# Row maxima turned by VectorE in 32x32 blocks, a later first block for them, another order of the split products, and VectorE's low parts one slot later

## The reference, cut to what matters

```python
x  = L0_attn_z                                  # (4, 1024, 128)
xn = layernorm(x)
# attention over xn: second layernorm with weights, 16 heads of width 8
qkv    = (zn @ W_qkv + b_qkv)
scores = einsum('bhqd,bhkd->bhqk', q, k) * 8 ** -0.5
s      = xn + softmax(scores) @ v ... @ W_proj + b_proj
# experts over xn: 8 experts of hidden size 512, the two best of 8 weighted
h   = gelu(einsum('td,edh->eth', xn, W1) + b1)
ffn = einsum('etd,te->td', einsum('eth,ehd->etd', h, W2) + b2, weights)
out = x + s * silu(ffn)
```

## Time and profile before

| | |
|---|---|
| median of 3 runs | 1103.75 us (1102.54 to 1105.91) |
| profiled execution | 1103.0 us |
| its span, first to last instruction | 1101.2 us |
| mean granted TensorE clock | 0.988 |
| TensorE busy | 1029.3 us, 93% |
| VectorE busy | 883.7 us, 80% |
| ScalarE busy | 866.9 us, 79% |
| GpSimd busy | 368.0 us, 33% |

### The profile page before, as it was taken

The page is one execution under the profiler, slowest core; times in us unless marked ns, Lnnn a source line. Parts: engine busy times, 40 slices in busy tenths (PEclk is TensorE's granted clock), DMA queues, the critical chain, the costliest instruction groups (busy, mean ns, idle before and its releaser), DMA issues.

```text
span 1101.2 us, 17451 instructions
## 1 busy us (share of the span) xinstructions
PE 1029.3 (93%) x5865; PEld 444.1 (40%) x5897; DVE 883.7 (80%) x1589; ACT 866.9 (79%) x1190; POOL 368.0 (33%) x555
## 2 busy tenths in 40 slices
PE   4998999999999999999999999999999999999997
PEld 3675666666666666664222222122222121122222
DVE  5647877787878787765999899989998998899943
ACT  6876667676767677666898998989898989798985
POOL 4786656657666667554001000001000001000010
PEclk9999999999999999999999999999999999999998
DMA  6432221414142232324212221212112221122102
GB/s 183 123 99 68 66 83 31 120 30 121 31 107 50 64 80 51 97 51 120 51 44 53 55 53 39 68 40 54 42 52 51 56 53 42 51 53 54 25 24 82
DMA packets 99410, 72.02 MB, mean 65 GB/s; under 512 B 21693, under 2 KB 83834, under 8 KB 99322
## 3 DMA queue, kind: packets, MB, share of 16 engines
q1 hardware_dynamic: 99322, 70.92, 24.5%
HBM read 53.12 MB, written 15.46 MB: 62 GB/s over the span
## 4 chain that ended last, share of the span: by engine, by line
PE 34%; ACT 8%; DVE 7%; issue 2%; SPq 1%; DMA 0%; POOL 0%; ACTq 0%; DVEq 0%; POOLq 0%
PE psum L1055 17%; PE psum L1034 8%; ACT p_ring L869 8%; PE psum L999 7%; DVE neg_max_half L1318 7%; PE psum L1084 1%; ACT o_sb L860 1%; DMA den<-o_sb 0%; SPq L469 0%; PE psum L1098 0%; PE psum L1010 0%; SPq L473 0%; DVE neg_max_rest L1327 0%; DVE y L1379 0%; POOL h_lo L685 0%
## 5 line engine op out<-in xcount | busy, mean ns | idle before, releaser
L869 ACT ACTIVATE p_ring<-psum 128x1024 f32<-128x1024 f32 x512 | 494.8, 1026 | 59.7 <-PE psum L1034 54.3
L1318 DVE TENSOR_REDUCE neg_max_half<-psum 128x1 f32<-128x512 f32 x768 | 481.6, 681 | 44.5 <-PE psum L999 36.7
L1055 PE MATMUL psum<-p_ring,v_sb 128*9 128x512 f32 x2048 | 269.2, 598 | 0.4 <-ACT o_sb L860 0.3
L823 ACT ACTIVATE h_hi<-psum,cols 128x512 fp32r<-128x512 f32 x192 | 132.4, 690 | 132.2 <-PE psum L949 131.2
L999 PE MATMUL psum<-k_max_stack,q_max_stack 48*128 48x512 bf16 x768 | 202.2, 380 | 16.6 <-DVE neg_max_half L1318 16.3
L1336 DVE TENSOR_REDUCE neg_max_half<-psum 128x1 f32<-128x512 f32 x256 | 169.3, 683 | 51.7 <-PE psum L985 45.0
L685 POOL TENSOR_TENSOR h_lo<-h_split,h_hi 128x512 fp32r<-128x512 f32 x128 | 165.1, 1294 | 135.4 <-ACT h_split L826 135.2
L1034 PE MATMUL psum<-q_stack,k_stack 51*128 51x512 bf16 x1024 | 200.0, 386 | 3.4 <-ACT p_ring L869 2.2
L635 POOL CAST neg_max_parts<-neg_max_rest 128x16 bf16<-128x16 f32 x32 | 6.3, 197 | 493.6 <-DVE neg_max_rest L1327 493.5
L1034 PEld LDWEIGHTS psum<-q_stack,k_stack 51*128 51x128 bf16 x1024 | 49.5, 93 | 299.2 <-ACT p_ring L869 276.2
L947 PE MATMUL psum<-xn_t_hi,w_hi 128*128 128x512 f32 x256 | 144.8, 566 | 0.7 <-DVE neg_max_half L1336 0.5
(11 more groups left out here) (129 smaller groups left out, 957.5 us busy)
## 6 DMA issues: line engine op xcount, KB each, us to landing
expert_w_bc<-expert_w_dram SPq DMA_DIRECT2D x64, 256.0 KB, 5.1
k_rows_dram<-qk_parts SPq DMA_DIRECT2D x24, 256.0 KB, 3.1
q_max_stack<-q_rows_dram SPq DMA_DIRECT2D x64, 96.0 KB, 2.5
k_max_stack<-k_rows_dram SPq DMA_DIRECT2D x64, 96.0 KB, 2.5
q_stack<-q_rows_dram SPq DMA_DIRECT2D x64, 96.0 KB, 2.4
k_stack<-k_rows_dram SPq DMA_DIRECT2D x64, 96.0 KB, 2.5
q_rows_dram<-qk_parts SPq DMA_DIRECT2D x8, 384.0 KB, 2.6
xz<-in_L_attn_z_dram SPq DMA_DIRECT2D x8, 256.0 KB, 3.2
```

Source lines behind the costliest of these rows:

```text
L823: act.activation(hh[:, (g * HS + j) % HR, :], up, ACT.Gelu, bias=col(C_B1 + i))\
L869: act.activation(p_sb[:, n % PR, a, :, :].rearrange("p h t -> p (h t)"), scores_bank[s % 2], ACT.Exp, scale=SCALE).then_inc(S("P"), 1)
L1055: i = pe.matmul(o_bank[at:at + VR, :], v_sb[:, b * KT + kt, 2 * (p % PB) + hh, :], p_sb[:, n % PR, a, hh, :], start=(kt == 0), stop=(kt == ...
L1318: dve.tensor_reduce(mx[:, p % MXR, c, hh * NT + t:hh * NT + t + 1], ring_bank(("max", u)), AX.X, ALU.max, negate=True).then_inc(S("R"), 1)
```

## The change

1. TensorE's turn of the maxima and ScalarE's copy go. VectorE turns the parts in 32x32 blocks from SBUF to SBUF (`max_turn`): the parts' tile is padded to four parts, 64 columns, so each partition block of 32 holds the transpose of its own tokens. The store writes 128 rows of 128 bytes. The load puts the pieces in order: six DMAs per pair, each of 32 pieces of 64 bytes, instead of two. The turns take no bank of the ring any more, and stand three blocks, or seven slots, after the pair's last reduction.
2. The 768 maxima products of the attention stage are spread over blocks 2 to 239 instead of 0 to 239. The zeroing of the O bank moves into the last group of the expert stage.
3. Of the three split products, low weights by high data comes first, so that the two products of the same high weights follow one another.
4. VectorE's low parts of h stand one slot later in its plan.

The second identity (`ident_b`) and its waits go as well. The diff, cut to its core:

```diff
-    NM = 2 * PARTS * NT
...
-    m_dram = nc.dram_tensor("neg_max_dram", (PAIRS, NM, P), BF16, kind="Internal").ap()
+    m_dram = nc.dram_tensor("neg_max_dram", (PAIRS, P, 2 * VC), BF16, kind="Internal").ap()
...
-        nmp = sb("neg_max_parts", [P, 2, 2, PARTS, NT], BF16)
-        nmT = sb("neg_max_t", [NM, 2, P], BF16)
+        nmp = sb("neg_max_parts", [P, 2, 2, VC // NT, NT], BF16)
+        nmT = sb("neg_max_t", [P, 2, 2 * VC], BF16)
...
+        MAX_FROM = 2
...
-            upto = [min(len(SINGLES), -(-((n + a) * len(SINGLES)) // MAX_BLOCKS)) for a in range(2)]
+            upto = [min(len(SINGLES), -(-max(0, n + a - MAX_FROM) * len(SINGLES) // (MAX_BLOCKS - MAX_FROM)))
+                    for a in range(2)]
...
-        turn_at = {done_block(p) + 2: p for p in range(EARLY_PAIRS, PAIRS)}
+        turn_at = {done_block(p) + 3: p for p in range(EARLY_PAIRS, PAIRS)}
...
-            turns = []
-            if n in turn_at:
-                turns.append(("mT", turn_at[n]))
-            return halves, turns
+            return halves
...
-        EARLY_TURN = [2 * HT + 2, 2 * HT + 28, 3 * HT + 26, 4 * HT + 26, 5 * HT + 26, 6 * HT + 26, 7 * HT + 5, 8 * HT + 1]
         EARLY_MIN = [d + 2 for d in EARLY_DONE]
+        EARLY_TURN = [d + 7 for d in EARLY_DONE]
...
-            kind, k = RING[at][:2]
-            if kind == "max":
-                eng.wait_ge(S("R"), EARLY + k + 1)
-            else:
-                eng.wait_ge(S("mTc"), k + 1)
+            eng.wait_ge(S("R"), EARLY + RING[at][1] + 1)
...
-            sp.wait_ge(S("mTc"), p + 1)
+            sp.wait_ge(S("mT"), p + 1)
...
-                sp.dma_start(q_s[HALF * hh + QROWS:HALF * hh + SROWS, slot, :],
-                             m_dram[p].rearrange("(h i t) c -> h i (t c)", h=2, i=PARTS)[hh])\
-                    .then_inc(S(f"m_ld{slot}"), 16)
+                src = m_dram[p, :, VC * hh:VC * (hh + 1)].rearrange("(b i t) c -> i t b c", b=P // VC, t=NT)
+                for i in range(PARTS):
+                    row = HALF * hh + QROWS + i
+                    sp.dma_start(q_s[row:row + 1, slot, :].rearrange("a (t b c) -> a t b c", t=NT, c=VC), src[i:i + 1])\
+                        .then_inc(S(f"m_ld{slot}"), 16)
...
+            pool.memset(nmp[:, :, :, :, :], 0.0).then_inc(S("pool"), 1)
...
-            def neg_max_t(p, early=False):
-                m_tr = (b5 if early else ring_bank(("mT", p)))[0:NM, 0:P // 2].bitcast(BF16)
-                act.wait_ge(S("mT"), p + 1)
-                if p > 1:
-                    act.wait_ge(S(f"m_st{p % 2}"), 16 * (p // 2))
-                act.activation(nmT[:, p % 2, :], m_tr, ACT.Copy).then_inc(S("mTc"), 1)
...
-                    turned = sum(t < (g - 1) * HT + 9 for t in EARLY_TURN)
-                    if turned:
-                        pe.wait_ge(S("mTc"), turned)
...
-                        pe.matmul(o, w1h[:, e, ws], G(xh, g), start=True, stop=False)
-                        pe.matmul(o, w1l[:, e, ws], G(xh, g), start=False, stop=False)
+                        pe.matmul(o, w1l[:, e, ws], G(xh, g), start=True, stop=False)
+                        pe.matmul(o, w1h[:, e, ws], G(xh, g), start=False, stop=False)
                         pe.matmul(o, w1h[:, e, ws], G(xl, g), start=False, stop=True).then_inc(S("h"), 1)
...
-                        pe.matmul(o, w2h[:, e, ws], hh[:, at, :], start=(c == 0), stop=False)
-                        pe.matmul(o, w2l[:, e, ws], hh[:, at, :], start=False, stop=False)
+                        pe.matmul(o, w2l[:, e, ws], hh[:, at, :], start=(c == 0), stop=False)
+                        pe.matmul(o, w2h[:, e, ws], hh[:, at, :], start=False, stop=False)
                         hl_done(pe, g, i)
...
-            def m_t(p, early=False):
-
-                pe.wait_ge(S("nmp"), p + 1)
-                if early:
-                    pe.wait_ge(S("wT"), min(NG, (EARLY_TURN[p] - 22) // HT + 2))
-                else:
-                    ring_free(pe, ("mT", p))
-                m_tr = (b5 if early else ring_bank(("mT", p)))[0:NM, 0:P // 2].bitcast(BF16)
-                pe.transpose(m_tr, nmp[:, p % 2, :, :, :].rearrange("p h i t -> p (h i t)"), ident_b[:, :])\
-                    .then_inc(S("mT"), 1)
...
-                for _, k in turns:
-                    m_t(k)
...
                     if split(i) and by_vector(i):
-                        plan.setdefault(i, []).append(low_h(i))
+                        plan.setdefault(i + 1, []).append(low_h(i))
...
+            def max_turn(p):
+
+                dve.wait_ge(S("nmp"), p + 1)
+                if p > 1:
+                    dve.wait_ge(S(f"m_st{p % 2}"), 16 * (p // 2))
+                dve.transpose(nmT[:, p % 2, :], nmp[:, p % 2, :, :, :].rearrange("p h i t -> p (h i t)"))\
+                    .then_inc(S("mT"), 1)
...
-            beside = {}
+            def o_zero():
+
+                dve.wait_ge(S("vd"), NG)
+                dve.memset(o_bank[:, :], 0.0).then_inc(S("o_zero"), 1)
+
+            beside = {(NG - 1) * HT + 2: [o_zero]}
...
                 beside.setdefault(EARLY_MIN[p], []).append(lambda p=p: half_min(p))
+                beside.setdefault(EARLY_TURN[p], []).append(lambda p=p: max_turn(p))
...
-            dve.memset(o_bank[:, :], 0.0).then_inc(S("o_zero"), 1)
...
                     row_max(u)
+                if n in turn_at:
+                    max_turn(turn_at[n])
                 if p > 0 and kt == 5:
                     head_rden(p - 1)
```

More of the change, by code:

```diff
@@ L111, in attention_and_experts @@
         ident = sb("ident", [P, P])
-        ident_b = sb("ident_b", [P, P], BF16)
         cols = sb("cols", [P, 64])
@@ L214, in block_items @@
             halves = [[("max", u) for u in range(singles_upto(n, a), singles_upto(n, a + 1))] for a in range(2)]
-            turns = []
-            if n in turn_at:
-                turns.append(("mT", turn_at[n]))
-            return halves, turns
+            return halves
         for n in range(BLOCKS):
-            halves, turns = block_items(n)
-            for item in halves[0] + halves[1] + turns:
+            halves = block_items(n)
+            for item in halves[0] + halves[1]:
                 on_ring(item)
@@ L602, in _ @@
         def _(pool):
-            for n, t in enumerate((ident, ident_b)):
-                pool.memset(t[:, :], 0.0).then_inc(S("pool"), 1)
-                pool.wait_ge(S("pool"), n + 1)
-                pool.affine_select(out=t[:, :], in_=t[:, :], compare_op=ALU.not_equal, fill=1.0, base=0,
-                                   pattern=[[-1, P]], channel_multiplier=1).then_inc(S("ident"), 1)
+            pool.memset(ident[:, :], 0.0).then_inc(S("pool"), 1)
+            pool.memset(nmp[:, :, :, :, :], 0.0).then_inc(S("pool"), 1)
+            pool.wait_ge(S("pool"), 2)
+            pool.affine_select(out=ident[:, :], in_=ident[:, :], compare_op=ALU.not_equal, fill=1.0, base=0,
+                               pattern=[[-1, P]], channel_multiplier=1).then_inc(S("ident"), 1)
             ch = Chain(pool, S("pool_own"))
@@ L849, in _ @@
             prepare_first(pre, experts, {9: hi(range(2)), 12: hi(range(2, 4)), 18: hi(range(4, RAW))})
-            expert_phase(experts, pre, first={2 * (n - RAW) + 5: hi([n]) for n in range(RAW, 2 * E)},
-                         extra={EARLY_TURN[p] + 1: [lambda p=p: neg_max_t(p, early=True)] for p in range(EARLY_PAIRS)})
+            expert_phase(experts, pre, first={2 * (n - RAW) + 5: hi([n]) for n in range(RAW, 2 * E)})
             def o_copy(p):
@@ L870, in _ @@
                                    ACT.Exp, scale=SCALE).then_inc(S("P"), 1)
-                if n in turn_at:
-                    neg_max_t(turn_at[n])
                 if kt == 1 and p > 0:
@@ L883, in _ @@
         def _(pe):
-            pe.wait_ge(S("ident"), 2)
+            pe.wait_ge(S("ident"), 1)
             pe.wait_ge(S("rows"), 6 * 16)
@@ L994, in max_scores @@
                     pe.wait_ge(S("R"), EARLY)
-                    pe.wait_ge(S("mTc"), EARLY_PAIRS)
                     pe.wait_ge(S("vd"), NG)
@@ L1015, in _ @@
                 beside.setdefault(EARLY_AT[m], []).append(lambda m=m: early_scores(m))
-            for p in range(EARLY_PAIRS):
-                beside.setdefault(EARLY_TURN[p], []).append(lambda p=p: m_t(p, early=True))
             prepare_first(pre, experts)
@@ L1030, in scores @@
                     pe.wait_ge(S(f"st{slot}"), 64 * (p // 2 + 1))
-                    pe.wait_ge(S(f"m_ld{slot}"), 32 * (p // 2 + 1))
+                    pe.wait_ge(S(f"m_ld{slot}"), 2 * PARTS * 16 * (p // 2 + 1))
                 for hh in range(2):
@@ L1079, in project @@
                     pe.wait_ge(S("R"), EARLY + len(SINGLES))
-                    pe.wait_ge(S("mTc"), PAIRS)
                 wait(pe, "hn", 0, 0, g + 1)
```

## The result

The changed kernel takes 1090.03 us (median, 1088.04 to 1094.96), the kernel before 1104.38 us on the same chip (1102.54 to 1105.91). It is 14.3 us faster by the medians; the ratio of the runs is 0.9885, 95% interval 0.9853 to 0.9918. The forecast was 1084 us within 1073 to 1096: right in sign and inside the range, 6 us too hopeful.

A forecast was written before the change was run, and what follows sets the result against it. TensorE was taken as the bound (busy 1029.3 of 1101.2 us), stopping only for banks not freed. Savings of 9.6 us in attention and 10.3 in experts and seam, 19.9 together, gave 1084 us, range 1073 to 1096.

The forecast's parts named there:

- Turns off TensorE, -12.5 us: Attention stage: 24 turns leave TensorE, ScalarE and the ring, so their blocks become ordinary; 12.5 us saved (9.6 to 15.8).
- The upper end of 11 us: Attention stage: cost if a VectorE turn takes 0.63 us against 0.16 us of cover, 0.47 us each.
- rival 3: VectorE becomes the attention stage's bound: turns of 0.63 us cost 11 us, total 1096 us; chance 0.08.
- The DMA queue, 0 us: SP's queue: six maxima loads per pair instead of two take 2.9 us more but end before the scores; no cost.
- rival 4: SP's queue: maxima land late, TensorE waits at each pair's first scores; 1139 us at 1.2 us per issue; chance 0.04.
- Four-max blocks, +4.1: Attention stage: starting maxima at block 2 adds six blocks with four maxima at 0.69 us each; 4.1 us lost.
- Start, -1.2: Attention blocks 0 to 2, without maxima in the first two, take 7.5 us instead of 8.72; 1.2 us saved (0 to 3).
- Low parts a slot later, -7: Expert stage: VectorE no longer waits for ScalarE, so TensorE's stops at maxima shrink; 7 us saved (0 to 12).
- Rival 1: Expert stage: the later slot only moves the wait, to the down projection's third product; 7 us lost, 1091 us; chance 0.15.
- Early turns, waits and seam, -3.3: Expert stage: eight transposes leave TensorE, 1.2 us; waits for GpSimd's parts, 1.5; turn and copy at the seam, 0.6.
- Same weights in a row, 0: Expert stage: the second load of the same high weights is not left out, so the new product order gains nothing.
- Rival 2: Expert stage: the repeated weight load is left out, 8 us less, 1076 us; chance 0.11.

The follow-up runs named there:

- e9: e12 with the attention stage's maxima spread from block 0 again instead of block 2: 1078.37 us, ratio 0.9784.
- e5: The kernel before with only VectorE's low parts of h one slot later: 1094.47 us, ratio 0.9942.
- e6: The kernel before with only the product order changed, low weights by high data first: 1101.74 us, ratio 1.0009.
- e10: The kernel before with O rows issued first in their block, which left the order of issues as it was: 1101.5 us, ratio 1.0003.
- e11: e12 with each of the 24 attention turns on VectorE done three times: 1080.33 us, ratio 0.9804.
- e12: e3 once more, as base for further runs on another call: 1077.08 us, ratio 0.9771.
- e3: The changed kernel with the edits of both e1 and e2: 1077.51 us, ratio 0.9794.
- e8: The changed kernel with the old order of the split products: 1086.47 us, ratio 0.9877.
- e7: The changed kernel with VectorE's low parts back in their old slot: 1096.77 us, ratio 0.9942.
- e1: The changed kernel with SP issuing O rows and denominators first in their block: 1084.44 us, ratio 0.9855.
- e2: The changed kernel with maxima put in order by the store (four DMAs), so two DMAs load a pair: 1090.61 us, ratio 0.9915.
- e4: e1 with the attention stage's maxima spread from block 0 again: 1082.95 us, ratio 0.9838.

## Why the prediction was right, and where it was off

*Turns off TensorE, -12.5 us: right, but covered up by another term.* The fairest comparison is that of e9, where hardly anything is late on SP's queue (VectorE waits 1.0 us for denominators in all) and the maxima are spread as before, with e5, e6 and e10, whose attention stage is that of the kernel before: 523.35, 523.30 and 522.40 to 511.47, 10.9 to 11.9 us. The forecast had 12.5 (9.6 to 15.8). The duration of the turn on VectorE held, and its cover is wider than the 0.16 us of idle time ahead of one reduction: by e11 three turns in a row cost 0.13 us per pair beyond one. Nor is a turn in a block of four maxima "all paid": the six such blocks of e12 average 2.66 us, those without turn and minimum 2.64. The upper end of 11 us, and rival 3 with it, was too dark.

*The DMA queue, 0 us: this is the step that failed.* It cost 7 to 11 us by the profiles, 10 to 13 by the ratios of whole runs (0.9885 against 0.9794 and 0.9771). In the profiles e3 and e12 are 11.0 us shorter in blocks 4 to 239 than the changed kernel, 9.6 shorter than e8, and 7.4 than e7 (whose profile is its fastest run; the fault is in all three). The working compared the end of the six loads with the first scores of the pair, and took all that stands ahead of them on the queue as it was. Two things were left out. First, the new block numbers put the rows of maxima, or the store, ahead of the O rows in some pairs; the denominators then come up to 1.9 us late for VectorE, and TensorE stops behind it, for 2 us in block 134. Second, the loads of some pairs had less than the 5.7 us of slack of pair 25: with 0.69 us per issue rival 4's own formula gives -1.2 us for it, not late, but six pairs were late, by up to 1.3. In pair 28, the worst, the loads take 4.6 us instead of 0.6, and land 1.5 us behind their last issue, not 1.1; and from their start to the moment at which the scores could have begun there are 4.8 us instead of 5.4, as the turn that TensorE made in between is gone. In the pairs with the least slack the prediction's subtraction left "about zero", and a gain of 0.6 us in the blocks ahead of the scores, which its own first term claims, was not taken off. "Its cover is thin" was written, and the cover was not followed pair by pair. Rival 4 had the right queue, the smaller of its two places, and a price far too high. (The maxima of a pair are 12 KB, six loads of 2 KB, not six kilobytes; nothing hangs on it.)

e1 and e2 tell the two apart: the order of issues frees the reciprocal, the shorter load frees the scores, and only both together give the 11 us (6.0 and -1.7 alone). That the late denominators do the damage through VectorE and the ring is read from the trace. The fall of the clock is part of it, about 3 us where it happened, and the fault is there without it (e7, e8).

*Four-max blocks, +4.1: mis-sized.* 0.9 us (e9 against e12). Number and price of the added blocks were about right (3.7 us); what was missed is that the other four-max blocks become 2.5 us cheaper in sum. The working let the minimum, which leaves them, cancel against the turn, which enters six; in e12 the turns there cost nothing.

*Start, -1.2: right by the runs, though the first profile hid it.* Blocks 0 to 2 were to take 7.5 us instead of 8.72. They take 7.4 in e1, e2, e3, e7, e8, e11 and e12, 8.7 to 8.9 in the four profiles of the kernel before and its variants, 7.8 in the changed kernel's. How long TensorE's clock is low at the start blurs this: 3.41 us in some profiles, 6.83 in others, of either version. With 3.41 us blocks 0 to 3 take 10.7 and 10.8 us before (before, e5) and 9.4 to 9.7 in the seven; with 6.83 us they take 11.4 to 12.1 with maxima from block 0 (e4, e6, e9, e10) and 10.8 in the changed kernel. So the difference of 2.3 us between e9 and e12 is in part the clock. In the changed kernel's profile TensorE works with gaps between score pairs, where the maxima of the first two blocks stood before:

```profile
501.52 0.39 PE L1002 MATMUL psum<-q_stack,k_stack 51*128 51x512 bf16 x2 [0.21 <-ACT p_ring L856]
502.44 0.39 PE L1002 MATMUL psum<-q_stack,k_stack 51*128 51x512 bf16 x2 [0.53 <-ACT p_ring L856]
503.36 0.61 PE L1002 MATMUL psum<-q_stack,k_stack 51*128 51x512 bf16 x2 [0.53 <-ACT p_ring L856]
...
505.81 1.89 PE L1023 MATMUL psum<-p_ring,v_sb 128*9 128x512 f32 x8
```

and the table of windows gives this stretch a clock of 0.70 (6.83 us at 1.2 GHz from 503.3 on):

```profile
499.90:511.30 11.40, 9.62 (x46) 1.82 (x46) 5.81 (x9) 7.60 (x9) 1.27 (x1) 0.70 0.76 211
```

The same gaps stand in e12 (0.21 to 0.53 us), where the clock is low for 3.41 us; what decides between the two lengths is not shown. The saving was real and went into the longer slow stretch of that profile.

*Low parts a slot later, -7: right.* The first exponential comes at 499.9 to 503.5 us (mean 501.5) in the nine profiles with all edits of the expert stage (e8's without the order of products), at 507.9 with the low parts back, at 505.9 with this edit alone, at 511.4 to 514.6 (mean 513.1) in three profiles without it (before, e6, e10). So the slot is worth 6.5 to 7.2 us, with everything else or alone; among profiles with one and the same expert stage the mark varies by 3 to 4 us. TensorE's stops at the early maxima fell by about 6 us and ended at 6.5, not at 5 or less. Rival 1 is out.

*Early turns, waits and seam, -3.3: too small.* By the same means it is 4.5 to 5.2 us; which of its three parts is larger was not separated.

*Same weights in a row, 0: right*, by e6 and e8. Rival 2 is out.

Together, with the queue put right: 1077.1 us on a chip where the kernel before takes 1101.9. The 19.9 us of the forecast were there, and 5 more. So it is in part luck that the changed kernel lies only 6 us from the forecast: a term of about 10 us was put at nothing, and the 5 us by which the others together were sized too small made up for half of it.

## What to carry to other kernels

When a schedule written by block number is shifted, list for each in-order queue which issues now fall into the same block, pair by pair, and follow the transfer that has the least slack; an average slack says nothing of the block in which two of them meet. Small DMAs cost the issuing queue by their number: a reordering on the way to or from memory belongs on the side where it needs fewer issues, and what a reader waits for is issued first. After a large gain on paper that brings little, look at the single block times, not at their mean: here some ten late blocks held most of what had been saved over the others. And before a control run is read, compare the order of issues in both traces: an edit can leave the program as it was.

## What the runs showed of the hardware

- One DMA of 32 pieces of 64 bytes holds SP's queue for 0.69 us (4.17 us for six, up to 0.77), one of the two larger loads that it replaces 0.3 to 0.4. The Trainium skill (DMA: Bandwidth & Descriptors, Anatomy of one DMA), for the path through GpSimd, puts most of a small DMA's cost into completion; here the issues of one pair's maxima went from 0.77 to 4.17 us of the queue, and that part mattered as well.
- The time from issue to landing varies for the same DMA: the median of the denominator pieces is 1.7 us, one took 3.0 us in the changed kernel (six loads issued behind it) and one 3.75 us in the kernel before (two loads behind it). The cause is open.
- A 32x32-block transpose of 128x64 bf16 takes VectorE 0.20 to 0.25 us.
- Short stops of TensorE can be followed by a slower clock, and need not be: in block 94 of the changed kernel, after stops of 1.22 and 0.20 us, it was granted 1.2 GHz for 3.41 us at once, in block 134, after a stop of 1.96 us, from 2.3 us later on. A stop of 1.33 us at the scores of pair 28 was not followed by it, nor were stops of 1.32 and 1.81 us in e7, and of 1.22 and 2.28 us in e8, at the same two blocks.
